# One TensorE-bound kernel, another order of issue: SP's queue, x loads on ScalarE, bias additions and ring scaling moved on GpSimd

## What is computed

```python
style = s @ aff_w.T + aff_b
w_mod = w[None, :, :] * style[:, None, :]
demod = rsqrt(sum(w_mod * w_mod, axis=2) + EPS)
kx = x @ (w_mod * demod) + b            # q = k = v = kx, 16 heads of 32
A = softmax(q k^T / sqrt(32))           # 16 x 16 for each token
out = modulated_linear(A v, s, o_aff_w, o_aff_b, o_w, o_b)
```

## Time and profile before

| | us |
|---|---|
| timed runs (3) | 875.12, 877.69, 877.69; median 877.69 |
| the profiled execution | 876.58 |
| its span | 874.80 |
| TensorE busy | 798.3 |
| VectorE busy | 661.1 |
| ScalarE busy | 461.7 |
| GpSimd busy | 587.1 |
| mean granted TensorE clock | 0.976 |

### The profile page before, as it was taken

One profiled execution on the slowest core, in us unless ns is written; L12 is line 12 of the kernel. 1 busy time (PEld: TensorE's weight loads), 2 busy tenths in 40 slices (PEclk: granted clock), 3 DMA queues, 4 the chain that ended last, 5 costly groups with the idle time before them and its releaser, 6 DMA issues.

```text
span 874.8 us, 18776 instructions
## 1 busy us (share of the span) xinstructions
PE 798.3 (91%) x6938; PEld 644.5 (74%) x6938; DVE 661.1 (76%) x1077; ACT 461.7 (53%) x789; POOL 587.1 (67%) x763
## 2 busy tenths in 40 slices
PE   5996787999899999999899999999899999999986
PEld 5853565778677787878677788778677787878675
DVE  3589897878778686878868686878878686877652
ACT  3595545455464646455454746455564637464421
POOL 2379757677677676667778676677777675765542
PEclk9899898999999999999999999999999999999998
DMA  8972474556847566466847656566757465564441
GB/s 280 416 257 65 97 127 89 122 111 145 187 109 175 99 134 130 107 126 146 187 109 168 106 141 126 110 122 144 187 121 163 79 157 111 134 129 92 80 93 37
DMA packets 205739, 120.68 MB, mean 138 GB/s; under 512 B 174256, under 2 KB 179536, under 8 KB 203984
## 3 DMA queue, kind: packets, MB, share of 16 engines
q1 hardware_dynamic: 196432, 94.44, 49.1%
q0 software_dynamic: 4608, 16.78, 7.2%
q10 hardware_dynamic: 4608, 8.25, 3.0%
HBM read 69.60 MB, written 8.40 MB: 89 GB/s over the span
## 4 chain that ended last, share of the span: by engine, by line
PE 33%; DVE 16%; POOL 15%; SPq 12%; DMA 9%; issue 7%; ACT 6%; ACTq 1%; DVEq 0%; POOLq 0%
PE tok L466 15%; PE acc L466 13%; DMA oph<-fp 6%; SPq L343 4%; POOL fp L1767 3%; SPq L356 3%; SPq L330 3%; PE att L466 2%; POOL xlo L1713 2%; DVE q L1364 2%; PE xp L619 2%; POOL tok_s L1725 2%; DVE ytmp L1490 1%; DMA kb<-in_kb 1%; DVE norm L1476 1%
## 5 line engine op out<-in xcount | busy, mean ns | idle before, releaser
L1767 POOL TENSOR_TENSOR fp<-ytmp,fp 128x512 f16<-128x512 f32 x96 | 114.4, 1195 | 27.9 <-ACT fp L957 27.2
L957 ACT CAST fp<-ytmp 128x512 f16<-128x512 f32 x96 | 59.2, 617 | 133.9 <-DVE ytmp L1457 133.9
L466 PE MATMUL acc<-oph,W1hh 128*128 128x256 f16 x512 | 89.8, 280 | 9.1 <-DMA oph<-fp 8.4
L466 PE MATMUL acc<-opt,W1th 128*128 128x256 f16 x512 | 87.9, 277 | 5.0 <-DMA opt<-fp 5.0
L466 PE MATMUL acc<-ops,W1sh 128*128 128x256 f16 x512 | 84.9, 273 | 0.5 <-DMA ops<-fp 0.5
L466 PE MATMUL acc<-op0h,W1xh 128*128 128x256 f32 x256 | 74.3, 290 | 10.7 <-DVE op0l L1443 10.7
L466 PE MATMUL acc<-op0l,W1xh 128*128 128x256 f32 x256 | 73.1, 286 | 0.0
L466 PE MATMUL acc<-op0h,W1xl 128*128 128x256 f32 x256 | 73.0, 285 | 0.0
L466 PE MATMUL acc<-oph,W1hl 128*128 128x256 f16 x256 | 71.7, 280 | 0.0
L466 PE MATMUL acc<-opt,W1tl 128*128 128x256 f16 x256 | 70.8, 277 | 0.0
L466 PE MATMUL acc<-ops,W1sl 128*128 128x256 f16 x256 | 69.8, 273 | 0.0
(11 more groups left out here) (263 smaller groups left out, 2580.9 us busy)
## 6 DMA issues: line engine op xcount, KB each, us to landing
xsq<-in_x SPq DMA_DIRECT2D x32, 256.0 KB, 3.4
xb<-in_x SPq DMA_DIRECT2D x32, 256.0 KB, 3.1
out<-xb SPq DMA_DIRECT2D x32, 256.0 KB, 2.0
BD<-q SPq DMA_DIRECT2D x124, 64.0 KB, 2.1
BD<-v SPq DMA_DIRECT2D x124, 64.0 KB, 4.7
xraw<-in_xT SPq DMA_DIRECT2D x30, 256.0 KB, 3.7
ring<-in_k_wT ACTq DMA_DIRECT2D x6, 256.0 KB, 3.8
dmb<-dm_rows SPq DMA_DIRECT2D x6, 256.0 KB, 4.8
```

The source lines that it names most:

```text
L466: return e.matmul(o, a, b, start=start, stop=True, skip_group_check=True)
L957: e.copy(fp[slot][:, 0, :], ytmp[YT[n, g][0]][:, :]).then_inc(s[f"o{n}h"], 1)
L1767: e.tensor_tensor(f[:, 1, :], ytmp[YT[n, g][0]][:, :], f[:, 0, :], ALU.subtract).then_inc(s[f"o{n}l"], 1)
```

## The change

None of the edits changes what is computed:

- SP: `blocks_v(b)` goes ahead of `store(pb-2)` and `turn(pa, h)`, and both stores and token loads are set anew; `load_ids` is one DMA of a host-made [128, 256] array instead of four broadcasts, and goes behind `blocks_v(a+2)`; `load_x` and `load_sq` leave SP.
- ScalarE issues `load_x` and `load_sq`.
- GpSimd: `add_be` of two groups leaves the end of a step for the next one, behind `affine(pb)`; `mod_scale(2, 3)` goes from behind `prod_lo(pb, s)` to ahead of `x_lo(a+2)`.
- First step: the low part of W1's h goes from VectorE (`low_16`) to GpSimd (`lo_16`), after ScalarE has scaled raw_h in place (`scaled_h`); `scaled_hi("h")` goes ahead of the loop; the W2 low parts go behind `root2(a)`; `product(1, t)` and `prod_hi(1, t)` go earlier, `split3(1)` goes ahead of `product(2, t)`.
- TensorE, step 15 alone: `values(b)` and `gains(a, t)` go behind the first half of W1's h, `a_T(b)` behind its end.

```diff
@SP
-                t = slice(k * 256, k * 256 + 256)
-                for i, n in enumerate(("cid", "sid", "bid", "cid")):
-                    e.dma_start(ids[quad(i), :], A[n][t].partition_broadcast(32)).then_inc(s["ids"], 16)
+                e.dma_start(ids[:, :], A["ids"][k]).then_inc(s["ids"], 16)
...
-                if more:
-                    load_x(a + 2)
-                    load_sq(a + 2)
                 turn(pb, "t")
                 if k > 1:
                     store(pa - 2)
                 if front:
                     blocks_q(b)
-                if k > 1:
-                    store(pb - 2)
-                    if front:
-                        load_tok(a)
+                if front and k > 1:
+                    load_tok(a)
                 if k == 1:
                     turn(pa, "s")
                 turn(pb, "s")
-                if front and k > 1:
-                    load_tok(b)
+                if front:
+                    blocks_v(b)
+                if k > 1:
+                    store(pb - 2)
                 turn(pa, "h")
                 if mod_of(k + 1):
                     load_rows(*mod_of(k + 1))
-                if more:
-                    load_sq(b + 2)
-                if front:
-                    blocks_v(b)
-                if more:
-                    load_ids(k + 1)
-                    load_x(b + 2)
                 turn(pb, "h")
+                if front and k > 1:
+                    load_tok(b)
                 if more:
                     blocks_q(a + 2)
...
                 if more:
                     blocks_v(a + 2)
+                    load_ids(k + 1)
@TensorE
-                if front:
+                if more:
                     values(b)
                     gains(a, "t")
...
                     W1_part(k - 1, "h", 0)
+                    if front and not more:
+                        values(b)
+                        gains(a, "t")
                     W1_part(k - 1, "h", 1, (0,))
-                    if front:
+                    if more:
                         a_T(b)
                     W1_part(k - 1, "h", 1, (1,))
+                    if front and not more:
+                        a_T(b)
@ScalarE
+            def load_x(g):
+
+                if g:
+                    e.wait_ge(s["A"], g)
+                e.dma_start(xraw[:, :, :], A["xT"][g]).then_inc(s["ldx"], 16)
+
+            def load_sq(g):
+
+                if g:
+                    e.wait_ge(s["sqx"], g)
+                e.dma_start(xsq[:, :], A["x"][g * 128:g * 128 + 128, :]).then_inc(s["lsq"], 16)
+
+            def scaled_h():
+
+                w = raw["h"][:, :, :].rearrange("p a b -> p (a b)")
+                e.wait_ge(s["wh"], 7)
+                e.activation(w, w, ACT.Copy, scale=beta).then_inc(s["nst"], 1)
...
             squares(3)
+            load_sq(4)
...
             z_make(1)
+            scaled_hi("h")
             exponential(2)
...
                 if front:
+                    if k == 1:
+                        prod_hi(pb, "t")
                     q_hi(b)
...
                 if k > 1:
                     prod_hi(pb, "t")
+                if more:
+                    load_x(a + 2)
                 if front:
                     e_first(a)
                 if k == 1:
-                    prod_hi(pb, "t")
                     e.wait_ge(s["pa"], 1)
                     e.activation(t2[:, 0:256].bitcast(BF16), rp[:, :], ACT.Copy, scale=up).then_inc(s["tp"], 1)
-                    scaled_hi("h")
+                    scaled_h()
...
                     squares(a + 2)
+                    load_sq(b + 2)
...
                         q_hi(a + 2)
+                        load_x(b + 2)
                     e_first(b)
+                    if k == 1:
+                        e.wait_ge(s["tA"], 2)
+                        e.copy(t2[:, 256:512].bitcast(BF16), rp[:, :]).then_inc(s["tp"], 1)
                     z_make(a)
...
                         squares(b + 2)
-                    if k == 1:
-                        e.wait_ge(s["tA"], 2)
-                        e.copy(t2[:, 256:512].bitcast(BF16), rp[:, :]).then_inc(s["tp"], 1)
+                        if a + 4 < NG:
+                            load_sq(a + 4)
@VectorE
-                if k > 1:
-                    product(pb, "t")
+                product(pb, "t")
...
                     if k == 1:
-                        low_16("h", (0, 1))
-                        low_16("h", (2, 3))
+                        split3(1, rp[:, :], PT[:, :])
                     product(a, "t")
                     v_stats(a)
                     a_sum(b)
-                    if k == 1:
-                        split3(1, rp[:, :], PT[:, :])
@GpSimd
                 prod_lo(pb, "t")
                 affine(pb)
+                if k > 1 and front:
+                    add_be(pa)
+                    add_be(pb)
                 if not front:
                     root3(pb - 2)
                 root2(pb)
+                if mod_of(k):
+                    mod_scale(*mod_of(k), (2, 3))
                 if more:
                     x_lo(a + 2)
                     bounds(a + 2)
...
                 prod_lo(pb, "s")
-                if mod_of(k):
-                    mod_scale(*mod_of(k), (2, 3))
                 prod_lo(pa, "h")
+                if k == 1:
+                    e.wait_ge(s["nst"], 9)
+                    lo_16("h", s["wlp"], (0, 1))
...
                 prod_lo(pb, "h")
                 if k == 1:
-                    e.wait_ge(s["wh"], 8)
-                    split_lo(WL["2", "l"], raw["2"], WL["2", "h"], s["wlp"], (0, 1))
+                    lo_16("h", s["wlp"], (2, 3))
                 if front:
                     root1(a)
                     affine(a)
                     root2(a)
                     if k == 1:
+                        e.wait_ge(s["wh"], 8)
+                        split_lo(WL["2", "l"], raw["2"], WL["2", "h"], s["wlp"], (0, 1))
                         split_lo(WL["2", "l"], raw["2"], WL["2", "h"], s["wlp"], (2, 3))
-                        add_be(0)
-                        add_be(1)
...
                     root1(b)
+                    if k == 1:
+                        add_be(0)
+                        add_be(1)
...
-                if more:
-                    add_be(a)
-                    add_be(b)
```

More of the change, by code:

```diff
@@ L668, in W1_part @@
                 if k == 0:
-                    e.wait_ge(*{"x": (s["wlx"], 1), "t": (s["wlp"], 1), "s": (s["wlx"], 2), "h": (s["wlx"], 3)}[n])
+                    e.wait_ge(*{"x": (s["wlx"], 1), "t": (s["wlp"], 1), "s": (s["wlx"], 2), "h": (s["wlp"], 2)}[n])
                 if n == "x":
@@ L680, in W1_part @@
                         if k == 0 and n == "h" and kt == 2:
-                            e.wait_ge(s["wlx"], 4)
+                            e.wait_ge(s["wlp"], 3)
                         oh, ol = (op[0]["h"][:, kt, :], op[0]["l"][:, kt, :]) if n == "x" else (opT[n][:, :, kt, :], opT[n][:, :, 4 + kt, :])
@@ L704, in W2_part @@
                 if g < 2:
-                    e.wait_ge(s["wlp"], 2 + ms[0] // 2)
+                    e.wait_ge(s["wlp"], 4 + ms[0] // 2)
                 e.wait_ge(s["asl"], 2 * (g // 2) + ms[0] // 2 + 1)
@@ L1445, in one_hot @@
             def one_hot(k):
-                e.wait_ge(s["ids"], 64 * (k + 1))
+                e.wait_ge(s["ids"], 16 * (k + 1))
                 if k > 1:
@@ L1757, in add_be @@
                 xs = xb[g % 4]
+                if g == 0:
+                    e.wait_ge(s["c_rp"], 32)
                 e.wait_ge(s["xTr"], rows_done(g))
                 e.wait_ge(s["z"], g + 1)
-                if g == 0:
-                    e.wait_ge(s["c_rp"], 32)
                 e.tensor_tensor(xs[:, :], xs[:, :], beint[:, :], ALU.add).then_inc(s["xbe"], 1)
@@ L1958 @@
     arr["int_w2"] = blocks(L1("int_W2"))
-    arr["cid"] = c(get("itok_BxS_0_4").reshape(-1))
-    arr["sid"] = c(get("mask_BxS_ik0").reshape(-1))
+    cid, sid = get("itok_BxS_0_4").reshape(-1), get("mask_BxS_ik0").reshape(-1)
     arr["pidx"] = c(get("itok_BxS_0_999").reshape(NG, 128).T)
-    arr["bid"] = np.repeat(np.arange(4, dtype=np.int32), 1024)
+    bid = np.repeat(np.arange(4, dtype=np.int32), 1024)
+    quarters = np.stack([cid, sid, bid, cid]).astype(np.int32).reshape(4, 1, NT, 256)
+    arr["ids"] = c(np.broadcast_to(quarters, (4, 32, NT, 256)).reshape(128, NT, 256).transpose(1, 0, 2))
     p = np.arange(128)
```

4 lines of the change are left out of this document (2 added, 2 removed).

## The result

The changed kernel takes 893.37 us (median; 887.47 to 896.96) against 877.69: the ratio is 1.0167 with a 95% interval of 1.0123 to 1.0211, so 1.2 to 2.1% slower. The forecast was 868.4 and the range ended at 881. The profiled execution took 891.23 us with a span of 889.3; against 876.58 that is 14.65 us more.

What follows compares the result with a forecast made beforehand. TensorE, busy 91% of the span, was taken as the bound. Step 1 -6.7, plain steps -4.7, rescale steps +1.5 and step 15 with the end +1.7 gave -8.2 from 876.58: 868.4 us, range 853 to 881.

Steps and rivals of the forecast that it cites:

- part 1: SP's order, ids and x loads: h transpose issued earlier, landing after 4.1 us; plain steps' oph 3.61, BD 2.13 waits go.
- 3a to 3c: Six rescale steps: oph waits go (3.27), V waits beyond e12 go (1.6), half-clock loss in steps 3 and 7 returns (2.6).
- part 2: GpSimd's add_be behind affine(pb): opt waits go (1.56 us), finish comes late, new alo wait of 0.37 us per plain step.
- part 3d: mod_scale(2, 3) moved ahead in six rescale steps: contended VectorE makes e12 1.5 us late each, 9.0 in all.
- part 4: Step 1: W1h low part leaves VectorE, PT made earlier, first W2 matmul 137.5 instead of 144.22: -6.7 us.
- part 5: Step 15 and end: values(b) behind half of W1h, waits on h transpose and a_T(b): +1.7 us (-0.5 to +3).
- part 3: Six rescale steps together: oph, V and half-clock gains against e12 late by mod_scale's move: +1.5 us (-15.3 to +10).
- both rivals: GpSimd and VectorE without contention, 847 us, chance 0.22; or taking strict turns, 886 us, chance 0.15.
- e12: VectorE's result at the end of the softmax chain, awaited by TensorE's values(b); forecast 1.5 us late per rescale step.
- second rival: GpSimd and VectorE take strict turns in six rescale steps, e12 2.5 us late: +13 there, 886 us, chance 0.15.
- The first sign: Step 5 at 47.0 us or less with no oph or BD wait would show part 1 right.

Runs made afterwards that it cites:

- b_xid: The kernel before with only the x loads moved to ACT's queue and the ids in one load behind blocks_v(a + 2): ratio 0.9900, 869.48 us.
- n_sp: a_three_back with only SP's new order put back in: ratio 1.0053 to the kernel before, 883.4 us.
- f_be: a_four_back with only the two add_be moved from the end of the step before to behind affine(pb): ratio 0.9842 to the kernel before.
- f_mod: a_four_back with only mod_scale(2, 3) moved ahead of x_lo: ratio 0.9883 to the kernel before.
- a_four_back: a_three_back with TensorE's order of before in step 15, leaving first-step part, single ids load and x loads on ACT: ratio 0.9792, 859.20 us.
- a_three_back: The changed kernel with mod_scale, add_be and SP's order all undone: ratio 0.9812 to the kernel before, 861.29 us.
- a_mod_back: The changed kernel with mod_scale(2, 3) again behind prod_lo(pb, s): ratio 1.0090 to the kernel before.
- n_tok: n_sp with store(pb - 2) and load_tok(b) at their old places; that is a_three_back with the V blocks alone moved ahead of turn(pa, h): ratio 0.9948.
- f_dmb: a_four_back with load_rows moved from ahead of the V blocks to right ahead of turn(pb, h): ratio 0.9884 to the kernel before.
- f_adj: a_four_back with turn(pa, h) moved to right ahead of turn(pb, h): ratio 0.9837 to the kernel before.
- a_sp_back: The changed kernel with SP's queue in the order of before, x loads staying on ACT and ids in one load: ratio 0.9978.
- n_sp_split: n_sp with turn(pa, h) ahead of the V blocks and store(pb - 2): ratio 0.9909 to the kernel before.
- n_quiet: n_tok with load_rows also moved behind blocks_q(a + 2): ratio 0.9996 to the kernel before.

## Why the prediction was wrong, point by point

By the parts of the sum, in us against before:

| part of the prediction | predicted | measured by |
|---|---|---|
| x loads, ids out of turn(pb, h)'s way (parts 1, 3a to 3c) | -13.2 | -8.8 (b_xid) |
| V blocks ahead, h transposes adjacent, store, load_tok, load_rows (part 1) | 0 | +21.2 (n_sp) |
| add_be (part 2, with the opt waits) | +1.0 | +4.4 (f_be) |
| mod_scale (part 3d) | +9.0 | +8.0 (f_mod) |
| step 1 (part 4) | -6.7 | -9.5 (a_four_back), -7.9 in the traces |
| step 15 and the end (part 5) | +1.7 | +1.8 (a_three_back), within the error |
| sum | -8.2 | +17.1; the whole change: +14.7 |

The first row is 5.7 (the plain steps without the opt waits) and 7.5 (3.27 + 1.6 + 2.6). The measured parts add up to the whole within their errors, of 2 to 6 us each. That they come out a little above it would fit waits in series that cover each other, as in a_mod_back; it is not shown.

**The step that failed** is in part 1: "it issues at about 328.9 and lands 4.1 us (median; 3.1 to 6.1) later, at 333.0". The issue was right in the plain steps, where turn(pb, h) goes out 1.3 to 2.6 us earlier than before. The landing was not: it took 6.0 us in the median. The 4.1 us was read in another order, and was carried over to the new one. Not that the transpose had been alone there; this is the kernel before, step 6:

```profile
378.30 0.48 SPq L312 DMA_DIRECT2D xraw<-in_xT  x1
378.88 2.31 SPq L356 DMA_TRANSPOSE oph<-fp  x1
```

A 256 KB x load went out 0.5 to 0.8 us ahead of it in steps 1 to 14, behind four small ids loads and the V copies, and it landed after 4.1 us all the same. One such load directly ahead does not make it late. What the changed kernel has besides is the other h transpose 3.1 us ahead or less (7.2 to 8.8 before), the store between V copies and transposes, in six steps the dmb load between the two transposes, and load_tok(b) directly behind. n_sp shows that this order alone costs 21.2 us; n_tok, f_dmb and f_adj show parts of it, and which property of the order lengthens the landing stays open. The range of the earlier trace rows was even quoted, but its upper end, 6.1, was taken for scatter.

Moving the V blocks "some 2 us earlier" was priced as a gain for V alone. That turn(pa, h) now stands behind their wait for v_T has no sentence in the prediction; in the rescale steps it goes out at +24.3 to +25.4, where it went out at +17.7 before. There turn(pb, h) is late in issue too, at +26.7 to +27.0 instead of +24.9 to +26.0, since VectorE's product comes late (part 3); a_sp_back, with SP's order of before, has +26.7 to +26.8 as well. Neither has this a rival: both rivals were about GpSimd and VectorE.

**Part 1, plain steps.** V waits gone: right, but not by moving the V blocks, as b_xid is rid of them without that. oph waits gone: right for x loads and ids alone (0.6 us in b_xid), wrong for the whole. ACT's queue: b_xid shows no cost, and in the loop of the changed kernel ACT waits for xraw only twice, 0.55 us in step 1 and 0.94 in step 13, below the 1 us that was named as a sign.

**Part 2.** The mechanism was right, and finish measured 1.76 where 1.29 was taken. (0.75 less the slack of 0.42 is 0.33, not 0.37; nothing hangs on it.) The slack was read on one chain only: alo waits came out at 0.2 to 0.3 in steps 2, 5, 9 and 15 (0.37 predicted), but SP's stores, V copies and transposes shifted as well.

**Part 3.** The price of mod_scale's move, 1.5 us a step, was right (1.7 in f_mod's trace, 1.3 by the ratios). In the whole change it was more: product(pa, h) came at +15.0 us in step 7, where it came at +12.6 before, and e12 2.2 later. The second rival, strict turns, said 2.5, and +13 for these steps; +15.9 came, but not by its mechanism alone. (The bounds of this part do not agree with each other: the upper one is +10 in the sum and +7.5 in the paragraph behind it, and the lower one comes to -15.6.) Over a_three_back these steps cost 14.1 with the two GpSimd moves (a_sp_back) and 13.1 with SP's order (n_sp), and 23.4 with both. The Trainium skill, page SBUF — State Buffer, section "Who interferes with whom", which spoke against this change, is borne out in kind: an instruction of 0.75 us beside a product of 1.26 took 1.26 to 1.77. The size lies between the forecast's 1.5 us a step and the 2.5 of strict turns: in step 7 of f_mod values(b) starts at +29.6 instead of +27.8.

**Part 4.** a_T(3) at 130.91 behind a wait on ET of 2.12 (131.2 and about 4 predicted), first W2 matmul at 135.74 (137.5 predicted), against 144.22 before:

```profile
130.91 0.66 PE L610 MATMUL xp<-ident,ET 128*128 128x128 f32 x4 [2.12 <-DVE ET L1437]
```

**Part 5.** The sum was right by two errors that met: step 15 cost 3.9 us (its oph wait was 3.52, again a late landing), and the stretch behind it became 2.4 shorter.

**What would show it.** Of the signs named, the alo waits (0.3, and 1.6 in rescale steps), 52 us rescale steps for the second rival, and the half clock in a new place (steps 6 and 11) came; the last was named as what makes the prediction wrong. The first sign nearly came as well, and would have misled: step 5 took 47.40 us without a wait on oph or BD, though its transpose landed after 5.7 us. It is one of two plain steps that stayed without the wait, the other being step 2; a part of seven steps is not judged by one.

## What to carry to other kernels

A transfer's landing time read from a profile belongs to the order in which it was read: when that order is changed, take the landing from a place in the trace where the same neighbours stand, or price the upper end of its range where there is no such place, and price each transfer that ends up behind a new wait. Work of an off-path engine can be moved into a gap of its own and still cost on the path, if it falls beside another engine's instructions with two inputs in SBUF, as GpSimd's beside VectorE's here; a shift of the whole engine moves all that hangs on it, SP's queue too, not only the one consumer with known slack. And a change of six parts may hold two good ones: here a_four_back, with only x loads, ids and first step kept, is 2.1% faster than before (interval 1.7 to 2.4%).

## What the runs showed of the hardware

**Landing of a transposing DMA.** The same 128x1024 half-precision transpose took 3.0 to 3.3 us at the end of the loop, in step 16. As turn(pb, h) of steps 2 to 15 it took 3.4 to 5.8 us in the kernel before and 3.3 to 5.6 in a_three_back; 4.7 to 7.7 in the changed kernel, 4.0 to 7.8 in n_tok, 3.8 to 6.4 in f_adj and up to 8.0 in n_sp_split. The ranges overlap, so a single landing proves little. SP's own instruction for it, mostly 1.25 us long, grew too: to 3.48 us in step 12 of the changed kernel and to 4.17 in step 4 of n_sp, and what SP issues next waits behind it. The Trainium skill, page DMA: Bandwidth & Descriptors, section "Queues, rings and completion order", says that a completion count is written only after every earlier write from the same DMA engine, across its queues. The 11.6 us landing in n_quiet agrees with that, as the gather issued 0.2 us ahead of the transpose landed at the same moment (283.3); a 256 KB x load issued beside them landed after 5.1 us, and none of the runs separates this from plain sharing of bandwidth.

**A phase that tips.** In step 12 of f_adj, VectorE stood 0.59 us for ScalarE's SE, which it did not in a_four_back. VectorE's mod_lo(0, 1) then came 0.66 us later in the step and GpSimd's mod_scale(2, 3), at its old place, 0.81 us earlier, and they fell onto each other. VectorE's two mod_lo, GpSimd's two products and finish in f_adj:

```profile
647.79 2.31 DVE L1255 SCALAR_TENSOR_TENSOR Wol<-ring,styl,Woh 128x512 f16<-128x512 f32 x2
...
649.50 3.41 POOL L1718 TENSOR_TENSOR raw_o<-raw_o,dmb 128x512 f32<-128x512 f32 x2
...
650.02 1.77 DVE L1515 SCALAR_TENSOR_TENSOR xb<-ytmp,norm,xb 128x512 f32<-128x512 f32 x1
```

In a_four_back the same take 1.51, 2.51 and 0.74. alo was 2.5 us late, from shifts of 0.7 and 0.8. f_be shows the same in its step 12 (52.1 us instead of 49.0), behind an opt wait of 0.77. So a small shift can cost more than itself here. It may be part of why a late transfer costs more than its own wait, and of why the times of one kernel spread by 5 us and more (no run shows that).
